# A decoder layer in one kernel: the cross-attention exponentials stay in the PSUM bank of their scores until they are normalised

## What is computed

```
qx  = ln(linear(ln_out, wqx))             # b, 112, 8 groups, 2 heads, 128
kx, vx = split(cond @ w_kv_x.T)           # b, 375, 8 groups, 128;  kx = ln(kx)
scores = einsum('bsghd,btgd->bghst', qx, kx) / sqrt(128)     # 112 x 375 for each head
p   = softmax(scores, axis=-1)
out = einsum('bghst,btgd->bsghd', p, vx)
```

## Time and profile before

| | us |
|---|---|
| median of 3 runs | 1210.69 (1209.44 to 1211.73) |
| the profiled execution, its own time | 1207.03 |
| its span in the trace | 1205.2 |
| PE busy | 1147.8 (95%) |
| DVE busy | 913.0 (76%) |
| ACT busy | 820.2 (68%) |
| POOL busy | 603.5 (50%) |

### The profile page before, as it was taken

The page is one execution under the profiler, slowest core; times in us unless marked ns, Lnnn a source line. Parts: engine busy times, 40 slices in busy tenths (PEclk is TensorE's granted clock), DMA queues, the critical chain, the costliest instruction groups (busy, mean ns, idle before and its releaser), DMA issues.

```text
span 1205.2 us, 20369 instructions
## 1 busy us (share of the span) xinstructions
PE 1147.8 (95%) x6330; PEld 764.5 (63%) x6330; DVE 913.0 (76%) x2769; ACT 820.2 (68%) x2348; POOL 603.5 (50%) x753
## 2 busy tenths in 40 slices
PE   4889989789999999999999999999999998999998
PEld 2566767456666665676666676667676666554564
DVE  4569979999888876698797878758887896586242
ACT  4667668787877886578776776667876678566140
POOL 1547975644544564265354654435654462357172
PEclk9979989899999999999999999999999999999999
DMA  8210010212111221213223220123411200000000
GB/s 275 89 60 25 27 33 17 87 54 70 54 36 36 62 83 31 87 55 101 68 75 105 79 88 23 57 70 120 126 50 45 66 14 1 2 1 1 35 1 27
DMA packets 28588, 70.39 MB, mean 58 GB/s; under 512 B 3024, under 2 KB 10320, under 8 KB 28480
## 3 DMA queue, kind: packets, MB, share of 16 engines
q1 hardware_dynamic: 28208, 68.72, 18.1%
q10 hardware_dynamic: 272, 0.36, 0.1%
HBM read 61.73 MB, written 7.34 MB: 57 GB/s over the span
## 4 chain that ended last, share of the span: by engine, by line
PE 70%; DVE 12%; ACT 7%; POOL 7%; issue 3%; DMA 1%; ACTq 0%; SPq 0%; POOLq 0%; DVEq 0%
PE ps L945 19%; PE ps L1042 8%; PE ps L937 8%; PE ps L1013 8%; PE ps L997 6%; PE ps L971 6%; PE ps L1054 4%; PE ps L980 4%; PE ps L957 3%; ACT big L1276 2%; DVE big L1415 2%; POOL big L1767 1%; POOL big L1765 1%; PE ps L864 1%; POOL big L1756 1%
## 5 line engine op out<-in xcount | busy, mean ns | idle before, releaser
L945 PE MATMUL ps<-big 128*125 128x512 bf16 x1152 | 264.7, 379 | 1.3 <-ACT big L1335 0.8
L1276 ACT ACTIVATE big<-ps,big 112x128 f32<-112x128 f32 (+1 forms) x512 | 192.8, 456 | 64.2 <-POOL big L1793 63.1
L1791 POOL TENSOR_TENSOR big<-big 112x4 f32<-112x4 f32 (+1 forms) x128 | 41.0, 320 | 340.5 <-ACT big L1108 340.4
L945 PEld LDWEIGHTS ps<-big 128*125 128x125 bf16 x1152 | 155.0, 136 | 82.0 <-ACT big L1335 1.2
L937 PE MATMUL ps<-big 128*112 128x512 bf16 x768 | 187.5, 388 | 2.2 <-ACT big L1310 1.2
L937 PEld LDWEIGHTS ps<-big 128*112 128x112 bf16 x768 | 99.8, 132 | 66.9 <-issue 7.0
L1335 ACT ACTIVATE big<-ps,big 112x375 f32<-112x375 f32 x128 | 74.9, 586 | 79.9 <-DVE big L1603 79.8
L1620 DVE TENSOR_SCALAR big<-big 112x112 f32<-112x112 f32 (+1 forms) x256 | 122.4, 499 | 6.8
L1415 DVE BATCH_NORM_STATS2 big<-ps 112x6 f32<-112x128 f32 (+1 forms) x512 | 113.2, 283 | 18.3 <-PE ps L945 11.4
L997 PE MATMUL ps<-big 125*128 125x224 f32 (+1 forms) x512 | 120.1, 357 | 5.8 <-DVE big L1639 4.1
L971 PE MATMUL ps<-big 128*112 128x375 f32 x256 | 102.8, 483 | 0.4 <-ACT big L1276 0.4
(11 more groups left out here) (124 smaller groups left out, 2318.3 us busy)
## 6 DMA issues: line engine op xcount, KB each, us to landing
big<-in_ctx_t SPq DMA_DIRECT2D x32, 375.0 KB, 3.3
big<-in_w_s SPq DMA_DIRECT2D x16, 512.0 KB, 3.7
big<-in_w_p SPq DMA_DIRECT2D x16, 512.0 KB, 3.7
big<-in_w_x SPq DMA_DIRECT2D x16, 512.0 KB, 3.7
big<-in_w_g SPq DMA_DIRECT2D x16, 512.0 KB, 4.1
big<-in_w_d SPq DMA_DIRECT2D x8, 512.0 KB, 4.2
scr<-big SPq DMA_DIRECT2D x28, 128.0 KB, 1.7
big<-scr SPq DMA_DIRECT2D x7, 512.0 KB, 8.3
```

Source lines behind the costliest of these rows:

```text
L945: t = e.matmul(bk[0:CK, :], ctxT[:, s, k, CK * c:CK * c + CK], wt[:, u, k, col:col + 512], start=k == s == u == 0, stop=k == 3 and s == 1)
L1276: t = e.activation(z[0:rows, 128 * j:128 * j + 128], ps(("p_mm", n))[0:rows, 128 * j:128 * j + 128], ACT.Identity, bias=v["q"][:, j:j + 1] ...
```

## The change

The exponentials of a cross-attention head are written back over the scores in their PSUM bank, and DVE's product reads them from there. The self-attention halves keep their SBUF buffer. The bank is given back by the signal of the product (`pn_made`) in place of that of the exponentials (`exp_made`), and its `give` stands in step `t_s1`, one tick later in the list.

```diff
@@ place()
         elif s == "t_s0":
             bank.take((s, k))
             att_small.take((s, k))
-            bank.give((s, k), exp_made[k])
+            if ATT[k][3] is None:
+                bank.give((s, k), exp_made[k])
         elif s == "t_s1":
             att_small.give(("t_s0", k), pn_made[k])
+            if ATT[k][3] is not None:
+                bank.give(("t_s0", k), pn_made[k])
@@ scalar_program, t_s0
-                t = e.activation(p[0:T, 0:SC], bk[0:T, 0:SC], ACT.Exp, bias=sm[0:T, 0:1], accum_out=sm[0:T, 2:3])
+                t = e.activation(bk[0:T, 0:SC], bk[0:T, 0:SC], ACT.Exp, bias=sm[0:T, 0:1], accum_out=sm[0:T, 2:3])
@@ vector_program, t_s1
-                dst, src = pn[0:T, wide * j:wide * j + wide], p[0:T, wide * j:wide * j + wide]
+                dst, src = pn[0:T, wide * j:wide * j + wide], ps(("t_s0", n))[0:T, 0:SC]
```

## The result

| | median us | runs | ratio to before, 95% interval |
|---|---|---|---|
| before, same chip | 1211.21 | 4 (1209.44 to 1213.51) | |
| after | 1228.16 | 4 (1226.67 to 1232.76) | 1.0145 [1.0113, 1.0177] |

Slower, as forecast, but by 17 us where 7.6 were predicted. The time is 0.16 us above the upper end of the range. The profiled execution of after took 1228.16 us as well, so its trace is of the median run; that of before took 1207.03, some 4 us less than its median.

A forecast was written before the change was run, and what follows sets the result against it. PE was taken to bound X0 and X1, so new waits for banks count in full. Each batch's first lateness less POOL's 0.44 us, plus X0/1's 1.2, summed to 7.6 us: 1218 us from a median of 1210.69, range 1209 to 1228.

The forecast's parts named there:

- raw lateness: Projections in X0 and X1: PE waits for `p_z` of the newly assigned bank, 0.54 us in X0/4, 0.81 at k1 of X1/2.
- The same product and POOL: End of `p_rstd`: a PSUM product no longer holds POOL, so q0's `p_z` comes 0.44 us earlier; 0.66 more freed in k1.
- No relief from POOL: Rival: POOL stays blocked, so each batch's largest lateness counts in full, 14.5 us slower, 1225 us; chance 0.14.
- all that follows on ACT comes 0.44 earlier too: ACT after q0's `p_z`: runs without a gap until `p_z` of q1, so the 0.44 us gain carries through.
- hidden by PE, worth 0: DVE's product from PSUM: 0.57 us against 0.67, 128 times, saves 13 us of DVE time but no kernel time.
- Within a batch I take the largest lateness, not the sum.: PE waits in X0 and X1: `p_z` times stay fixed when PE is late; adding up might cost up to 8 us more.
- X0/3: Batch X0/3: k1 was to start 2.49 us late for q1's `p_z`, net 2.05 us.
- X1/7: Batch X1/7: product with v 1.92 us late for the `t_s4` bank, taken up by later PE waits, net 0.
- ACT gets slower in PSUM: Rival: exponentials written to PSUM take 0.3 us more, delaying `p_z` at q1 and v0; 1224 us, chance 0.05.
- No difference: Rival: `p_z` comes still earlier than 0.44 us, the ten mild batches lose nothing; about 1212 us, chance 0.16.
- Faster: Rival: every lateness vanishes and DVE's and POOL's relief removes 3.1 us of PE waits ending X1; 1207.6 us, chance 0.10.

The follow-up runs named there:

- hold_only: Kernel before, SBUF buffer kept, with only the bank given back as in after, one tick later by the product's signal; 1223.89 us, ratio 1.0128.
- after_spacer: After, plus a one-number DVE reciprocal between the product and the operation that holds POOL; 1236.38 us, ratio 1.0221.
- after_reorder: After, with two DVE weight operations (`b_3`, `b_1`) moved ahead of the product in X0 and X1; 1234.36 us, ratio 1.0211.
- after_due: After, with a rule meant to hand out the bank due first; a wrong lookup key left the instructions unchanged; 1228.97 us, ratio 1.0164.
- dst_psum: After, but the product scales 112x375 constants in SBUF while the exponentials still go to the PSUM bank; ratio 1.0147.
- hold_reorder: hold_only with two DVE weight operations (`b_3`, `b_1`) moved ahead of the product in X0 and X1; 1248.41 us, ratio 1.0333.

## Why the prediction was right and wrong

**Right: what bounds it, and where the loss is.** PE had no slack; the sum that DVE saved in the product (86.2 to 77.8 us) bought nothing. The waits came at k1 and v0 for `p_z`, and nearly nowhere else. The estimates of the raw lateness were good where they were read from a batch of the steady kind: 0.54 us for X0/4, measured in hold_only as 0.58; 0.81 at k1 in X1/2, measured as 0.85.

**Wrong: "The same product and POOL".** This is the step of the prediction that failed: "Read from PSUM it should not", so 0.44 us earlier in each batch. The rows showed POOL held until the product *and* the short operations behind it were done, and I put the whole of it down to the product. after_spacer and after_reorder show that a PSUM product alone does not hold POOL (0.20 to 0.22 us beside it), and that a 128x256 operation on SBUF behind it does (0.57 to 1.13 us in after). So the sentence is right of the product by itself, and wrong of what POOL waits for here. With the 0.44 us gone, the sum is the rival "No relief from POOL", 14.5 us; hold_only measured 14.7 by its times and 16.3 in its trace. The 6.9 us between 7.6 and 14.5 are the larger part of the error. The second half of the step, "all that follows on ACT comes 0.44 earlier too", doesn't hold everywhere either: in X0/5 q1's exponential can't start before DVE's maximum is done, even if ACT is free. In after the maximum ends at 631.27 + 0.54 = 631.81, and the exponential starts at 631.84:

```profile
631.27 0.54 DVE L1606 TENSOR_REDUCE big<-ps 112x1 f32<-112x375 f32 x1
...
631.84 0.55 ACT L1338 ACTIVATE ps<-ps,big 112x375 f32<-112x375 f32 x1
```

A q0 that is earlier on ACT alone gains 0.03 us at most there. That k1's loss in the mild X0 batches rose in after_spacer with DVE's delay, though POOL was free, says the same.

The Trainium skill (SBUF — State Buffer, Who interferes with whom) says of GpSimd and a VectorE instruction in a two-port mode that whichever issues first gets the shared ports for the whole instruction and the other blocks. That either side can lose is what after and after_spacer show (POOL 0.85 and DVE 0.28 us; POOL 0.22 and DVE 0.73). The order of issue doesn't come out of the records: in after POOL's operation begins at 820.20 and L1547 at 820.69, and still POOL was the one that waited.

**Mis-sized: the product, "hidden by PE, worth 0".** Taken as 0.57 us, measured 0.608, within its bounds. But it isn't free. I compared it with the mean of 673 ns, while on the chain to `p_z` stands the quiet case of 0.41. Against that it is 0.20 us longer, and what waits behind it moves by 0.19: POOL's release in X1, DVE's next statistics and maximum in X0. That is the 3 us between hold_only and after. The Trainium skill's cycle table (VectorE: DVE Perf Modes, errata section) gave an estimate of 516 ns, which is too low by 92.

**Small: one lateness a batch.** "Within a batch I take the largest lateness, not the sum." In X1/2 the largest was to be 1.07 us, at v0, and hold_only lost 1.16. In X0/4 and X0/6 it lost 0.38 more at v1, behind the 0.6 of k1. Over all batches the differences between the rival's 14.5 us and the 16.3 of the trace go both ways (X0/3 -1.6, the six mild ones together +1.6, X1/7 +0.8). That its sum comes so near the measured times is in part luck.

**X0/3 and X1/7.** For X0/3, 2.49 us were read from PE's start and the end of `p_z`. But before had waits of its own in that batch, and in after PE reached k0 1.07 us *earlier* relative to the batch's start. q1's `p_z` ended 13.13 us after that start where it had ended 14.72 us after it, and the net was 0.62. X1/7's 1.92 was taken up as said (0.18 left).

**The rivals.** "ACT gets slower in PSUM" is refuted: the exponential became 28 ns shorter, 586 to 558, and with the destination alone 557. The Trainium skill (ScalarE: Activation LUTs, Step-by-step) calls PSUM the lower-latency destination, and the trace agrees. "No difference" and "Faster" rested on POOL's relief and fell with it.

## What to carry to other kernels

A buffer saved in SBUF by leaving data in PSUM is paid in banks: where PE is the bound and hands eight banks round in a fixed queue, look up which release the next user gets instead, since one bank held one tick longer cost 1.3% here with the same work on every engine. Before you count on POOL being freed by a change of one DVE instruction, look at the operation on SBUF behind it, and at what POOL will run in the time gained. When a chain crosses three engines, remove a wait on one and ask at once which of the others is next; here DVE's maximum ended only 0.03 us before the exponential started in a part of the batches. And an experiment has to change the instructions that are built, not only the code: after_due changed none, and its question is still open.

## What the runs showed that I had not expected

- POOL's operation on four numbers a row takes 0.85 us beside a PSUM product that has a 128x256 DVE operation on SBUF queued directly behind it, and 0.22 us beside the same product with a one-number reciprocal in between. A queued DVE instruction seems to take what it shares with POOL before its own record begins. The reciprocal's own form is not what frees POOL: with an operation that reads PSUM in its place (after_reorder) POOL takes the same 0.20 to 0.22 us.
- The other side of it: with POOL free to run on, DVE's two operations on 128x256 went from 312 to 511 and from 573 to 686 ns in the mean.
- The PSUM product takes 608 ns in all cases, where the SBUF product of before ranged from 0.41 us to over 1; its mean of 673 was the longer one.
- A new wait of PE can cost more than its length: in X0/3 of dst_psum 2.1 us of waiting were followed by matmuls at a granted clock of 0.50 and another 1.4 us lost, while hold_only kept its full clock after 2.0 us of waiting.
- One more short DVE operation behind each product, or the same operations in another order, cost 6 to 25 us on top of the held bank (after_reorder 1234.4 against after's 1228.2, hold_reorder 1248.4 against hold_only's 1223.9).
